# One block for all phases of a macaron layer, with the first two groups of rows loaded and normed in halves

## The reference

```python
x = x + 0.5 * ffn(layernorm(x))
x = x + attention(layernorm(x))
x = x + 0.5 * ffn(layernorm(x))
```

## Time and profile before

| | us |
|---|---|
| median of 3 runs | 2017.62 (2016.95 to 2019.78) |
| profiled execution | 2018.66 |
| its span, first to last instruction | 2016.9 |
| PE busy in the span | 1914.8 (95%) |
| DVE busy | 1399.0 (69%) |
| ACT busy | 653.6 (32%) |
| POOL busy | 279.0 (14%) |
| mean granted TensorE clock | 0.987 of full |

### The profile page before, as it was taken

The page is one execution under the profiler, slowest core; times in us unless marked ns, Lnnn a source line. Parts: engine busy times, 40 slices in busy tenths (PEclk is TensorE's granted clock), DMA queues, the critical chain, the costliest instruction groups (busy, mean ns, idle before and its releaser), DMA issues. The chain is left out here.

```text
span 2016.9 us, 29774 instructions
## 1 busy us (share of the span) xinstructions
PE 1914.8 (95%) x11600; PEld 1605.4 (80%) x11600; DVE 1399.0 (69%) x2733; ACT 653.6 (32%) x1176; POOL 279.0 (14%) x216
## 2 busy tenths in 40 slices
PE   2999999977999999999999999999999799999998
PEld 1788888856888888888888888888887678888886
DVE  5766667836777777777777777677778866665783
ACT  2543445624222222131222221221212244343552
POOL 3020101001011021020111110210201201010100
PEclk9999999998999999999999999999999899999999
DMA  6463445652111121121111120211211336433565
GB/s 220 136 210 124 106 152 172 188 177 88 30 30 41 21 55 25 16 56 23 27 43 29 40 40 12 59 21 20 53 19 35 105 128 205 134 97 126 163 187 183
DMA packets 189244, 181.33 MB, mean 90 GB/s; under 512 B 140336, under 2 KB 140336, under 8 KB 189104
## 3 DMA queue, kind: packets, MB, share of 16 engines
q1 hardware_dynamic: 181648, 162.09, 27.3%
q0 software_dynamic: 7456, 17.34, 4.2%
HBM read 137.40 MB, written 25.72 MB: 81 GB/s over the span
## 5 line engine op out<-in xcount | busy, mean ns | idle before, releaser
L1345 PE MATMUL at_pj<-at_w_lo,at_xT_hi 128*128 128x512 f32 x512 | 208.5, 407 | 0.0
L1345 PE MATMUL at_pj<-at_w_hi,at_xT_hi 128*128 128x512 f32 x512 | 200.6, 392 | 0.0
L1345 PE MATMUL at_pj<-at_w_hi,at_xT_lo 128*128 128x512 f32 x512 | 199.9, 390 | 0.0
L1319 PE MATMUL at_pj<-at_xT_hi,at_w_lo 128*128 128x512 f32 x384 | 157.3, 410 | 2.1 <-DVE at_xT_lo L1127 2.0
L606 DVE TENSOR_TENSOR last_ff_w_lo<-last_ff_stage,last_ff_w_hi 128x1024 fp32r<-128x1024 f32 x78 | 95.5, 1225 | 81.3 <-ACT last_ff_w_hi L430 81.3
L1319 PE MATMUL at_pj<-at_xT_lo,at_w_hi 128*128 128x512 f32 x384 | 151.4, 394 | 0.0
L1319 PE MATMUL at_pj<-at_xT_hi,at_w_hi 128*128 128x512 f32 x384 | 151.2, 394 | 0.0
L606 DVE TENSOR_TENSOR first_ff_w_lo<-first_ff_stage,first_ff_w_hi 128x1024 fp32r<-128x1024 f32 x78 | 96.1, 1232 | 72.0 <-ACT first_ff_w_hi L430 72.0
L906 POOL TENSOR_TENSOR at_w_lo<-at_stage,at_w_hi 128x1024 fp32r<-128x1024 f32 (+1 forms) x36 | 78.2, 2173 | 450.4 <-ACT at_w_hi L960 450.4
L1165 DVE TENSOR_TENSOR xres<-at_r,xres 128x512 f32<-128x512 f32 x128 | 88.6, 692 | 61.1 <-PE at_r L1410 59.9
L929 POOL TENSOR_TENSOR at_coef<-at_ms,minus_half 128x4 f32<-128x4 f32 x64 | 64.3, 1020 | 422.6 <-DVE at_ms L1276 422.6
(11 more groups left out here) (325 smaller groups left out, 4677.7 us busy)
## 6 DMA issues: line engine op xcount, KB each, us to landing
first_ff_stage<-wff SPq DMA_DIRECT2D x90, 512.0 KB
last_ff_stage<-wff SPq DMA_DIRECT2D x90, 512.0 KB, 3.6
at_turned_ke<-at_ke_blocks SPq DMA_DIRECT2D x496, 32.0 KB, 2.0
at_stage<-watt SPq DMA_DIRECT2D x24, 512.0 KB, 3.8
at_stage<-watt SPq DMA_DIRECT2D x16, 384.0 KB, 3.3
xres<-x SPq DMA_DIRECT2D x4, 1024.0 KB, 10.0
mid_rows<-xres SPq DMA_DIRECT2D x4, 1024.0 KB
out<-xres SPq DMA_DIRECT2D x4, 1024.0 KB
```

Source lines behind the costliest of these rows:

```text
L1319: last = pe.matmul(PJ[(7 * k + part) % 2][:, :], wq(w, kk, part), x[:, kk, tok], start=(kk == 0 and n == 0), stop=(kk == KC - 1 and n == 2))
L1345: last = pe.matmul(PJ[(7 * k + 3 + t) % 2][:, :], x[:, kk, tok], wvg(w, kk), start=(kk == 0 and n == 0), stop=(kk == KC - 1 and n == 2))
```

## The change

There is one block around everything. The phases give back one function per engine, and each engine calls them one after the other. Where the end of a block kept phases apart, there are now semaphore waits: DVE and PE wait for five constants at the start; SP waits for all the additions to `mid_rows` before it loads them for attention; in the last feed-forward ACT waits for the scatters of three groups before its first weight split, and SP before the second slot's load.

The first feed-forward loads group 0 tile by tile (the semaphores are shared with attention's, which therefore waits for 32), takes its statistics and norms in two halves, loads the router's rows behind group 1, and takes the first two gaps ahead of group 1's statistics. Attention norms unit 0 in two halves; on DVE `split_lo(0)` goes ahead of `row_statistics(1)` and `k_copy`, `s_clip` move each ahead by a place; on PE `project_s` goes ahead of `turn(1)`. In the last pair's last unit the tiles' statistics stand between the additions, and the last unit's statistics move behind the steps 0 and 1 of the last feed-forward.

```diff
-    with nc.Block() as block:
-        @block.gpsimd
-        def _(pool):
+    def program(pool):
...
-            pool.memset(c["ones"][:], 1.0)
-            pool.memset(c["minus_half"][:], -0.5)
+        pool.memset(c["ones"][:], 1.0).then_inc(const_done, 1)
+        pool.memset(c["minus_half"][:], -0.5).then_inc(const_done, 1)
...
+    def parts(g):
+        if g == 0:
+            return ((1, slice(0, RT // 2)), (2, slice(RT // 2, RT)))
+        return ((g + 2, tiles(g)),)
...
+            for i in range(RT):
+                sp.dma_start(xres[:, i, :], rows_in[:, i, :]).then_inc(norms["row_loaded"][i], 16)
+            for g in range(1, TILES // RT):
+                sp.dma_start(xres[:, tiles(g), :], rows_in[:, tiles(g), :]).then_inc(in_loaded[g], 16)
+                if g == 1:
                     sp.dma_start(rows[:, :, :], router...).then_inc(r_loaded, 16)
...
+        if early:
+            act.wait_ge(norms["scattered"], 16 * RT * (TILES // RT - 1))
         act.wait_ge(down_done, RING)
...
                     statistics(0)
                     dve.wait_ge(r_loaded, 16)
                     step(dve.tensor_tensor(wdiff[:], rows[:, 0, :], rows[:, 1, :], ALU.subtract))
+            step(gaps(0, range(0, RT // 2)))
                     statistics(1)
-                    route(0)
+            step(gaps(0, range(RT // 2, RT)))
+            choose(dve, step, r, tiles(0), is1_done)
+            mark(0)
                     route(1, before=0)
...
+        def late_statistics(t):
+            g = TILES // RT - 1
+            for i in range(g * RT + t * RT // 2, g * RT + (t + 1) * RT // 2):
+                last = dve.bn_stats(stats[:, i, :], xres[:, i, :])
+            if t == 1:
+                step(last)
+                for i in range(g * RT, (g + 1) * RT):
+                    last = dve.bn_aggr(mv[:, i, :], stats[:, i, :])
+                step(last)
+                dve.tensor_scalar(nmean[:, tiles(g)], mv[:, tiles(g), 0], -1.0, None, ALU.mult)
+                dve.tensor_scalar(vare[:, tiles(g)], mv[:, tiles(g), 1], EPS, None, ALU.add).then_inc(norms["var_ready"], 1)
         def beside(t):
+            if early and t < 2:
+                late_statistics(t)
...
         def sync_program(sp):
             from_mid = mid_rows.rearrange("(i p) d -> p i d", p=P)
+            sp.wait_ge(ahead["y_added"], ahead["all_added"])
...
             for m in range(UNITS):
-                pool.wait_ge(var_ready, m + 1)
+                for n, at in norm_parts(m):
+                    pool.wait_ge(var_ready, n)
...
             row_statistics(0)
-            row_statistics(1)
             split_lo(0)
-            row_statistics(2)
+            row_statistics(1)
             k_copy(0, 0)
-            split_lo(1)
+            row_statistics(2)
             s_clip(0, 0)
+            split_lo(1)
             row_statistics(3)
...
-                        add_out(*((i, k - 1) if k else (i - 1, UNITS - 1)), last_pair and k > 0 and more)
+                        add_out(*((i, k - 1) if k else (i - 1, UNITS - 1)), last_pair and k > 0)
...
-                    if not more:
-                        for cc in range(UC):
-                            tile_statistics(i, k - 1, cc)
...
-                        for cc in range(UC):
-                            tile_statistics(i, k, cc)
-                        unit_statistics(k)
...
             turned(0, 0, 1, k_mm)
-            turn(1)
             project_s(0, 0)
+            turn(1)
...
                         behind["first_turn"](pe, KC - 1, x_bank[KC - 1])
+                        pe.sem_inc(behind["down_done"], RING)
...
-        first["run"]()
...
-        last["run"]()
+        with nc.Block() as block:
+            @block.sync
+            def _(sp):
+                first["sync"](sp)
+                attention["sync"](sp)
+                last["sync"](sp)
...
```

More of the change, by code:

```diff
@@ L61 @@
 TO_OPERANDS = 80
+CONSTANTS = 5
 SQUARE = 32
@@ L172, in phase_feed_forward @@
     to_row = sb("ff_to_row", [P, 2, GT], I32)
-    in_loaded = [sem(f"rt_in_loaded{i}") for i in range(TILES // RT)] if x_in is not None else []
+    in_loaded = [None] + [sem(f"rt_in_loaded{i}") for i in range(1, TILES // RT)] if x_in is not None else []
     if x_in is not None:
@@ L752, with phase_attention @@
 HK_STEPS = [UC if k % HALVES == 0 else UC - 1 for k in range(UNITS)]
 HK_AT = [sum(HK_STEPS[:k]) for k in range(UNITS + 1)]
-def phase_attention(nc, top, c, watt, gnorm, mid_rows, slot_table, xres, norms, routing, sorted_rows, aw, behind):
+def phase_attention(nc, top, c, watt, gnorm, mid_rows, slot_table, xres, norms, routing, sorted_rows, aw, ahead, behind):
     with ExitStack() as ctx:
@@ L803, in phase_attention @@
         xn = [x[:, :, :].rearrange("p a b -> p (a b)") for x in (en, kn, ok)] + [pT[:, :]]
-        row_loaded = [sem(f"at_row_loaded{t}") for t in range(UC)]
+        row_loaded = norms["row_loaded"]
         rows_loaded = [sem(f"at_rows_loaded{m}") for m in range(1, UNITS)]
@@ L846, in phase_attention @@
         wo_mm, added = sem("at_wo_mm"), sem("at_added")
-        block = ctx.enter_context(nc.Block())
         NP = len(PIECES)
+        norms["var_ready"], norms["shift_done"], norms["scattered"] = var_ready, shift_done, scattered
         x_bank = [PJ[0], PJ[1], R[2], R[1]]
@@ L897, in _, with gpsimd_program @@
             behind["first_rows"](sp)
-        @block.gpsimd
-        def _(pool):
+        def gpsimd_program(pool):
             pool.sem_inc(coef_done, 1)
@@ L1110, in row_statistics @@
             def row_statistics(m):
[L1111 to L1122 removed]
+                for n, at in norm_parts(m):
+                    for t in range(at.start, at.stop):
+                        if m == 0:
+                            dve.wait_ge(row_loaded[t], 32)
+                        elif t == at.start:
+                            dve.wait_ge(rows_loaded[m - 1], 16)
+                        last = dve.bn_stats(bn[:, t % UC, :], xres[:, t, :])
+                    last.then_inc(bn_done, 1)
+                    dve.wait_ge(bn_done, n)
+                    for t in range(at.start, at.stop):
+                        last = dve.bn_aggr(mv[:, t, :], bn[:, t % UC, :])
+                    last.then_inc(mv_done, 1)
+                    dve.wait_ge(mv_done, n)
+                    dve.tensor_scalar(nmean[:, at], mv[:, at, 0], -1.0, None, ALU.mult)
+                    dve.tensor_scalar(vare[:, at], mv[:, at, 1], EPS, None, ALU.add).then_inc(var_ready, 1)
             def split_lo(m):
@@ L1536, in macaron @@
         norms["wdiff"] = wdiff
+        norms["row_loaded"] = [top.enter_context(nc.semaphore(f"row_loaded{t}")) for t in range(UC)]
         routing = {n: sb("rt_" + n, [P, TILES], I32 if n == "row_i" else F32) for n in (
@@ L1558, in macaron, with _ @@
         last["close"]()
-        phase_attention(nc, top, c, watt, gnorm, mid_rows, slot_table, xres, norms, routing, sorted_rows, aw, last)
-        last["run"]()
+        attention = phase_attention(nc, top, c, watt, gnorm, mid_rows, slot_table, xres, norms, routing, sorted_rows, aw, first, last)
+        with nc.Block() as block:
[4 more added lines that the diff above has]
+                last["sync"](sp)
+            @block.gpsimd
+            def _(pool):
+                c["gpsimd"](pool)
+                first["gpsimd"](pool)
+                attention["gpsimd"](pool)
+                last["gpsimd"](pool)
+            @block.scalar
+            def _(act):
+                first["scalar"](act)
+                attention["scalar"](act)
+                last["scalar"](act)
+            @block.vector
+            def _(dve):
+                dve.wait_ge(c["done"], CONSTANTS)
+                first["vector"](dve)
+                attention["vector"](dve)
+                last["vector"](dve)
+            @block.tensor
+            def _(pe):
+                pe.wait_ge(c["done"], CONSTANTS)
+                first["tensor"](pe)
+                attention["tensor"](pe)
+                last["tensor"](pe)
 def kernel(**inputs):
```

910 lines of the change are left out of this document (449 added, 461 removed).

## The result

The changed kernel takes 2009.92 us (median of six runs, 2008.51 to 2011.98), beside 2016.97 for the kernel before on the same chip: a ratio of 0.9966, 95% interval 0.9954 to 0.9978. A second comparison, on another chip, gave 0.9972 (0.9963 to 0.9982). That is 6 to 7 us faster, where 14.5 were forecast.

A forecast was written before the change was run, and what follows sets the result against it. TensorE, busy for 95% of the span, bounds the kernel, so only its idle time and slow clock can be had; 0 - 3.2 - 3.0 - 1.7 - 6.6 = -14.5 from 2018.66 gives 2004.2, 2003.1 like the median; forecast 2003.5, range 1999.0 to 2010.0.

The forecast's parts named there:

- term 3: Attention's start: halves, new order and clock bring unit 3's rows and the work forward; -3.0 us, bounds 1.2 and 5.0.
- Term 1: Kernel's start: SP issues 1.98 us earlier, but the router lands behind group 1; first scatter unmoved, 0, bounds -2.0 and +1.5.
- The four pieces: Rival at the kernel's start: group 0's four loads each pay the fixed DMA cost, +6 us, 2009; chance 0.04.
- Term 2: First feed-forward to attention: SP waits for the additions themselves, so its load goes out earlier; -3.2 us, lower bound 0.3.
- the drain is the landing: Rival at the first block's end: additions land only during POOL's drain, gain there 0.3 us, rest as forecast; 2006.4, chance 0.06.
- (a): Attention's start: with unit 0 normed in halves, ACT ends rows 2 and 3 at 462.25 instead of 463.27, 1.0 us earlier.
- (b): Attention's start: `split_lo(0)` follows ACT, not unit 1's statistics, 1.1 us more; first projection 2.1 us earlier.
- (c): Attention's next turns: q, k, s take 36 products, 8.2 us; ACT's order carries the rest, unit 3's rows 2.7 us earlier.
- (d): Clock at attention's start: PE's idle time before the first projection falls from 1.97 to about 1 us; 0.3 counted.
- Term 4: Attention's last unit: four statistics leave the chain before the norm and go between additions; -1.7 us, bounds 0.4 and 1.8.
- Term 5: Attention to last feed-forward: ACT's split waits for a scatter, PE's 3.60 idle goes, clock stays; -6.6 us, bounds 3.6 and 6.7.
- the cold starts: Rival: clock falls anyway, something else holds unit 3's turn, moved statistics stall PE once; gain 9.1 us, 2008.5, chance 0.14.

The follow-up runs named there:

- start_old: Changed kernel with attention's start as before: unit 0 normed as one group, old order on DVE and PE; 2009.73 us, ratio 0.9964.
- best2_stats_chain: Changed kernel plus POOL drain, router first, 90 ungated transposes and last-unit transposes, with unit 30's statistics back behind the scan of z; 2004.41 us, 0.9929.
- warm_end: Changed kernel with extra identity transposes in three PE waits of attention's last two units; 2006.91 us beside 2010.55 for the changed kernel.

## Why the prediction was wrong

The sum missed a term, POOL's drain at the kernel's end (+3.5 to +3.8 us), and counted term 3 as 3.0 where the changed kernel got 0 to 2 of it; terms 1 and 4 are off by less. Ten profiles give each stretch more than once. Each distance is between single rows of the timelines; the old code is in two of them, the new in four to eight:

```
stretch                                  before-code     changed-code      forecast
start to first scatter                   21.25, 21.35    21.3 to 22.05     0
last addition to SP's load               8.12            4.8 to 4.9        -3.2
SP's load to first copy into hk          51.4, 53.3      49.1 to 52.4      -3.0
attention's body                         1063.6, 1065.1  1063.3 to 1065.3  0
last unit's first product to first up    39.4, 41.7      37.9 to 42.3      -1.7
first up to 24 products later, to the    9.2 + 391.4     5.44 + 388.6      -6.6
  last scatter
last scatter to the end of the span      6.93            10.4 to 10.8      (none)
```

In the profiled pair alone, in the order of time, the differences are +0.70 and +0.14 (first scatter, rest of the first feed-forward), -3.22, -2.11, -1.65 (the body, which has a short slow stretch in the one and not in the other), +1.48, -3.76 and -2.28, +3.49: together -7.2, as the spans have it.

**Term 1, the start: +0.5 instead of 0.** The step "so it lands at about 0.8 + 10.0 = 10.8" failed. The router, last in line, was seen at 11.87 (11.1 to 11.9 over the runs). The bound of +1.5 held it. The four pieces did not cost 6 us. The Trainium skill (DMA: Bandwidth & Descriptors, "Anatomy of one DMA") gives about 2.0 us of fixed cost for one DMA, on the path of DMAs that GpSimd issues; added up for SP's four pieces, it does not give this start.

**Term 2: right, -3.2**, and the load is where I put it. The rival that the drain is the landing falls with it. It is also the term that misled me. I read the DRAIN of the earlier trace rows as a cost of the block's end that vanishes with the block. It was a debt per transfer, and the last block's end inherits it.

**The missing term, the tail: +3.5 in the profiled pair, +3.7 in the mean.** In the prediction the sum ends at the last feed-forward. I never followed POOL to the end of the kernel, and the trace of before held the contradiction: 2757, 1022 and 1757 ns for the same instruction with 33, 12 and 21 indirect transfers in front of it. The Trainium skill (VectorE: DVE Perf Modes, "The DRAIN you can't avoid") gives about 12 ns, on all engines, for the DRAINs ahead of and behind a program. At the four block ends of this trace DVE's own took 10, 24, 273 and 17 ns, and POOL's took 41 without transfers; with transfers the measurement decides.

**Term 3: less than 3.0.** Steps (a) and (b) held: the first projection is 12.22 us behind SP's load instead of 14.81, 2.6 less where 2.1 was forecast. Two steps of (c) and (d) failed. The first is "36 products, 8.2 us at 0.227": they took 10.8, since 13 of them ran 0.43 apart at half clock, where the kernel before has 8 such. I had moved them into the slow stretch that the earlier trace rows show until 464, and counted the clock as a gain of 0.3. The second is that ACT's order "then carries the rest" and brings unit 3's rows 2.7 us forward. From the last of the 36 products to these rows it takes 10.7 to 10.8 us in all eleven profiles with the new order on DVE and PE, and 8.2 in all six with the old: 2.6 us are given back, 1.7 of them by unit 1's turn, which now stands behind s. In the profiled pair the rows come 0.7 earlier (33.81 and 34.52); over the runs they are at 31.7 to 34.2 instead of 34.0 to 34.6.

The copies into `hk` differ by 1.8 on the average, with `start_old`'s 53.35 among the old ones. But they follow the time at half clock between the last addition and the copy: with 23.9 us of it the old order has 53.3 and the new 52.4, with 20.5 us 51.4 and 51.2 to 51.7, and the new with 17.1 us 49.1 and 49.8. At equal slow clock the term is worth 0 to 1 us, at full clock for the products perhaps 2.0.

**Term 4: about -0.7 instead of -1.7**, in the mean of the table, with a spread larger than the term; in the profiled pair it is +1.48. Its mechanism was right, as `best2_stats_chain` shows. What I left out is the clock, which falls in this unit before and after the change (17.0 and 23.9 us in the two old profiles, 10.2 to 23.9 in the new). At equal slow clock the mask `at_bm` starts 1.2 to 1.4 us earlier, but from there to the first up product it takes 19.9 to 21.5 us instead of 19.3 and 19.4. The last slow stretch there is twice as long in five of seven new profiles (6.8 us, not 3.4); whether that is all of it stays open. `warm_end` prices the clock of this unit at 3.6.

**Term 5: right, -6.6** (3.8 and 2.8), with ACT's wait let go by the scatter and no wait of PE behind `first_up(1)`.

The sum is 0.5 - 3.2 - 1.8 - 0.7 - 6.6 + 3.7 = -8.1 by the means, where the runs give 6 to 7. The rest may be what the first feed-forward differs by in the same code (its scatters end anywhere within 2.6 us). Of the rivals, the cold starts were right about the clock at attention's start and about unit 3's turn. They were wrong about the last feed-forward's start, which ran at full clock with no stall by the moved statistics and gained 6.6, not 3.6. That their 9.1 is only 2 us off is luck: this error and the missing term nearly cancel. The four pieces came nearest of all, 2009 beside 2009.92, and that is luck too: they put 6 us on the start, where the first scatter moved by 0.70. The signs that I had named: the first projection 12.2 us behind SP's load, as forecast; no idle time of PE behind `first_up(1)`, and no stall by `late_statistics`; the first scatter out by 0.70 instead of at most 0.5, and unit 3's turn moved by 3.9 against the first phase's last addition (44.04 to 40.12 behind it), less than the 4 that I had named.

## What to carry to other kernels

When a wait at a block's end is taken away, ask what the instruction there was paying for, and whether that is paid later. POOL's drain costs 82 ns per indirect transfer since the last one: give it a drain in the middle, where POOL is idle, right before the last few transfers. Where an engine's first work comes earlier, follow every queue for one unit further before counting the gain: here three engines took turns in holding the same point. And two profiles price an edit only if the slow clock lies over the same work in both.

## What was not expected of the hardware

The clock of TensorE moves times in pieces that a single profile can't tell from an edit: the same code's attention start took 49.6 us with 13.6 us of slow clock in front and 52.6 with 20.5, its last unit 37.9 with 10.2 and 42.3 with 23.9, and a short stretch of half clock near 1520 to 1530 us is there in some executions and not in others (1.8 us). Transposes of the identity in the last unit's waits left 3.4 us of slow clock there in five profiles, 6.8 in two and 10.2 in one, where without them it was 10.2 to 23.9. At attention's start 18 of them kept the clock up for all 36 products in one profile of five, and 90 of them, followed by an idle 3.43 us, did not. The router's 512 KB land 6.5 us after their issue ahead of group 1's megabyte and 8.7 us behind it, so this load waited for what had been issued before it.
